# Two attentions of a language-model tower: where the softmax is divided, and how two value parts are added

## What is computed

```
first (8 heads of 16):   A = softmax(logits, axis=-1)
                         out = einsum("bhnm,bhmd->bhnd", A, V);  out @ Wo + bo
second (8 heads of 64):  s = einsum("qhd,khd->qhk", q / sqrt(64), k)
                         e = exp(s - max(s));  num = e @ v;  den = e.sum(-1)
                         (num / den) @ w_out + b_out
```

## Time and profile before

| | |
|---|---|
| Median of three runs | 1261.18 us |
| The profiled execution | 1261.07 us, its span 1258.9 us |
| TensorE matmul, weight load | 1057.9 us (84%), 810.6 us (64%) |
| VectorE | 1018.2 us (81%) |
| ScalarE | 694.7 us (55%) |
| GpSimd | 478.0 us (38%) |

### The profile page before, as it was taken

The page is one execution under the profiler, slowest core; times in us unless marked ns, Lnnn a source line. Parts: engine busy times, 40 slices in busy tenths (PEclk is TensorE's granted clock), DMA queues, the critical chain, the costliest instruction groups (busy, mean ns, idle before and its releaser), DMA issues.

```text
span 1258.9 us, 24020 instructions
## 1 busy us (share of the span) xinstructions
PE 1057.9 (84%) x7816; PEld 810.6 (64%) x7816; DVE 1018.2 (81%) x3131; ACT 694.7 (55%) x1481; POOL 478.0 (38%) x459
## 2 busy tenths in 40 slices
PE   5587787888869988988988886899898988989997
PEld 4455555565547877877887786465565655667665
DVE  5797887978899999999999982885875876844777
ACT  2686768878533443344434431784774865825333
POOL 6672552616505424244324422360551624600000
PEclk9699998989978999999999998999999999989999
DMA  3310000000000000000000002000000000000000
GB/s 109 113 51 1 1 0 0 0 0 1 1 1 2 2 2 1 2 2 2 2 2 2 1 3 116 1 2 1 0 0 0 0 0 1 1 1 1 1 9 24
DMA packets 6424, 14.36 MB, mean 11 GB/s; under 512 B 1855, under 2 KB 4482, under 8 KB 5762
## 3 DMA queue, kind: packets, MB, share of 16 engines
q1 hardware_dynamic: 5314, 11.16, 2.5%
q0 software_dynamic: 1024, 2.10, 0.7%
HBM read 12.20 MB, written 1.05 MB: 11 GB/s over the span
## 4 chain that ended last, share of the span: by engine, by line
PE 31%; issue 30%; DVE 28%; POOL 5%; ACT 4%; DVEq 1%; DMA 0%; POOLq 0%; SPq 0%; ACTq 0%
PE quad L1492 5%; PE bank L1487 4%; PE quad L1186 4%; DVE a_eT L750 4%; DVE w_v L1001 4%; DVE i L918 4%; PE quad L1198 3%; PE quad L1390 3%; PE bank L1401 2%; PE bank L1334 2%; DVE one_u L1007 2%; POOL a_en L380 2%; POOL wu L361 2%; DVE bi L939 1%; PE bank L1370 1%
## 5 line engine op out<-in xcount | busy, mean ns | idle before, releaser
L380 POOL TENSOR_TENSOR a_en<-a_e,a_rrec 128x512 f32<-128x512 f32 x256 | 265.2, 1040 | 324.6 <-DVE a_rrec L744 307.5
L464 ACT ACTIVATE a_e<-bank,a_negmax 128x512 f32<-128x512 f32 x256 | 176.1, 688 | 72.0 <-DVE a_negmax L737 62.0
L737 DVE TENSOR_REDUCE a_negmax<-bank 128x1 f32<-128x512 f32 x256 | 175.9, 690 | 40.8 <-PE bank L1427 25.2
L1186 PE MATMUL quad<-ident,a_en 128*128 128x128 f32 x1024 | 164.2, 284 | 47.9 <-DVE a_eT L750 40.9
L1186 PEld LDWEIGHTS quad<-ident,a_en 128*128 128x128 f32 x1024 | 111.3, 143 | 139.0 <-issue 121.5
L406 POOL TENSOR_TENSOR vals<-relu_in,g_sb 128x512 f32<-128x512 f32 x80 | 125.9, 1610 | 156.3 <-DVE one_u L1007 120.1
L750 DVE TENSOR_TENSOR a_eT<-quad,a_eT 128x512 fp32r<-128x512 f32 x256 | 172.4, 676 | 4.1 <-ACT a_eT L473 4.1
L1198 PE MATMUL quad<-a_eT,a_v 128*128 128x512 f32 x512 | 173.0, 428 | 1.7 <-DVE a_eT L750 1.7
L1370 PE MATMUL bank<-xnT,wd 128*128 128x128 f32 x1024 | 137.4, 291 | 34.3 <-ACT relu_in L569 34.0
L473 ACT CAST a_eT<-quad 128x512 fp32r<-128x512 f32 x256 | 147.8, 577 | 23.7 <-PE quad L1186 19.7
L1370 PEld LDWEIGHTS bank<-xnT,wd 128*128 128x128 f32 x1024 | 127.1, 201 | 42.7 <-ACT relu_in L569 42.4
(11 more groups left out here) (221 smaller groups left out, 1852.7 us busy)
## 6 DMA issues: line engine op xcount, KB each, us to landing
wd<-in_pk_down SPq DMA_DIRECT2D x1, 2048.0 KB, 8.0
wu<-in_pk_up SPq DMA_DIRECT2D x1, 2048.0 KB, 12.6
wu<-in_moe_w SPq DMA_DIRECT2D x2, 1024.0 KB
out<-h SPq DMA_DIRECT2D x4, 256.0 KB, 2.3
wd<-in_num_rows SPq DMA_DIRECT2D x1, 512.0 KB
q_st<-in_pk_wqT SPq DMA_DIRECT2D x1, 512.0 KB
q_st<-in_pk_keys SPq DMA_DIRECT2D x1, 512.0 KB
wd<-in_a_wk SPq DMA_DIRECT2D x1, 512.0 KB
```

Of the source, the lines that this page charges most:

```text
L380: nc.gpsimd.tensor_tensor(m.en[:, s % 3, :], m.e[:, s % 3, :], m.rrec[:, s % 4:s % 4 + 1].to_broadcast([P, S]), ALU.mult).then_inc(a.nr, 1)
L464: nc.scalar.activation(m.e[:, s % 3, :], bank[LOGITS[s % 3]][:, :], ACT.Exp, bias=m.negmax[:, s % 4:s % 4 + 1], accum_out=m.rowsum[:, s % ...
L737: V.tensor_reduce(m.negmax[:, s % 4:s % 4 + 1], bank[LOGITS[s % 3]][:, :], AX.X, ALU.max, negate=True).then_inc(a.mx, 1)
L1186: last = tp(bank[2 + s % 2][:, c * P:(c + 1) * P], m.en[:, s % 3, c * P:(c + 1) * P], ident[:])
```

## The change

In the first attention the exponentials are no longer divided. TensorE transposes `a_e` itself, so GpSimd's multiplication goes, and the inverse of each unit's sum too. The row sums of 16 units are kept side by side and inverted at once (twice a batch); GpSimd spreads the inverses over 32 columns per head (`spread_sums`), TensorE transposes them in four pieces (`transpose_sums`, bank 7 or 2), ScalarE copies them to SBUF (`copy_rT`), and VectorE multiplies them onto the output bank (`outT0`) in place of ScalarE's copy. A buffer `a_e` is now free when its transposition is done (`tr`).

In the second attention ScalarE copies the high and the low value part of a head apart, 64 partitions each, so that two heads lie in one tile of 128 rows; GpSimd adds the two parts (`add_parts`, four a batch), and `wo1` holds each row once: four products for each token block in place of eight.

```diff
@@ GpSimd
+            def spread_sums(b, g):
+                pool.wait_ge(a0.rc, 2 * b + g + 1)
...
+                nc.gpsimd.tensor_tensor(mB.rspread[:].rearrange("p j a n -> p a j n"), ...
+                                        ALU.mult).then_inc(r_spread, 1)
+            def add_parts(b, pair):
+                pool.wait_ge(a1.ots, b * H + 2 * pair + 2)
+                nc.gpsimd.tensor_tensor(oT1[:, pair, :], o_parts[:, pair % 2, 0, :], o_parts[:, pair % 2, 1, :],
+                                        ALU.add).then_inc(o_added, 1)
...
+            spread_sums(0, 0)
             with pool.Fori(0, B - 1) as b:
-                normalise(a0, b, lnB)
-            normalise(a0, B - 1)
+                rstd_step(lnB, b + 1, TPB)
+                spread_sums(b, 1)
+                spread_sums(b + 1, 0)
+            spread_sums(B - 1, 1)
             rstd_step(lnC, 0, TPB)
...
             normalise(a1, B - 1)
-            with pool.Fori(0, B) as b:
+            rstd_step(lnE, 0, TPB)
+            last_parts(B - 1)
+            for b in range(1, B):
                 rstd_step(lnE, b, TPB)
@@ ScalarE
                     if s >= 3:
-                        act.wait_ge(a.nr, b * UNITS + s - 2)
+                        act.wait_ge(a.tr if a is a0 else a.nr, b * UNITS + s - 2)
...
-                    nc.scalar.copy(a.oT[:, g, :], bank[4 + g % 2]).then_inc(a.ots, 1)
...
+                        rows = slice(g % 2 * DH1, (g % 2 + 1) * DH1)
+                        nc.scalar.copy(o_parts[rows, g // 2 % 2, 0, :], bank[4 + g % 2][0:DH1, :])
+                        nc.scalar.copy(o_parts[rows, g // 2 % 2, 1, :], bank[4 + g % 2][DH1:P, :]).then_inc(a.ots, 1)
...
+                    if a is a0 and s == HALF_UNITS + 5:
+                        copy_rT(b, 0)
@@ VectorE
+            def outT0(b, g):
+                dve.wait_ge(rT_sb, 2 * b + g + 1)
+                dve.wait_ge(a0.pv, b * UNITS + (g + 1) * HALF_UNITS)
+                V.tensor_tensor(oT0[:, g, :], bank[4 + g % 2], mB.rT[:], ALU.mult).then_inc(a0.ots, 1)
...
+                    if a is a0 and s in (HALF_UNITS + 1, UNITS + 1):
+                        invert_half(s // HALF_UNITS - 1)
+                    if a is a0 and s == HALF_UNITS + 9:
+                        outT0(b, 0)
@@ TensorE
-                    pe.wait_ge(a.nr, b * UNITS + s + 1)
+                    pe.wait_ge(a.ex if a is a0 else a.nr, b * UNITS + s + 1)
...
+                    if a is a0 and s == HALF_UNITS + 4:
+                        transpose_sums(b, 0)
+                    if a is a0 and s == UNITS + 4:
+                        pe.wait_ge(a.lo, b * UNITS + UNITS - 1)
+                        transpose_sums(b, 1)
...
-                    for g in range(a.groups):
+                    for g in range(a.groups if a is a0 else H // 2):
```

More of the change, by code:

```diff
@@ L453, in copy_xnT, with copy_rT @@
                                bank[7][:, 0:n]).then_inc(ln.sb, 1)
+            def copy_rT(b, g):
+                act.wait_ge(rT_ps, 2 * b + g + 1)
+                nc.scalar.copy(mB.rT[:], bank[R_BANK[g]][:, :]).then_inc(rT_sb, 1)
             def attention(a, b, next_ln=None, n=None, dst=None, tail=None, early_ln=None):
@@ L485, in attention @@
                     done = s - 8
-                    if done > 0 and done % (TPB * a.group) == 0:
+                    if a is not a0 and done > 0 and done % (TPB * a.group) == 0:
                         outT(done // (TPB * a.group) - 1)
+                    if a is a0 and s == HALF_UNITS + 5:
+                        copy_rT(b, 0)
                     if s == UNITS + 4 and next_ln is not None:
@@ L510, in heads0 @@
                 nc.scalar.activation(table_out[:, 0:1], ones[0:1, 0:1], ACT.Sqrt)
+                if before is not None:
+                    copy_rT(before, 1)
                 act.wait_ge(dev_rdy, b + 1)
@@ L755, in attention @@
                         rowmax(s)
-                    if 0 <= s - 1 < UNITS:
+                    if a is not a0 and 0 <= s - 1 < UNITS:
                         invert(s - 1)
+                    if a is a0 and s in (HALF_UNITS + 1, UNITS + 1):
+                        invert_half(s // HALF_UNITS - 1)
+                    if a is a0 and s == HALF_UNITS + 9:
+                        outT0(b, 0)
                     if drained is not None:
@@ L825, in heads0 @@
                 V.tensor_tensor(dev, q4, wide(0), ALU.subtract).then_inc(dev_rdy, 1)
+                if before is not None:
+                    outT0(before, 1)
                 dve.drain()
@@ L1174, in transpose_xn, with transpose_sums @@
                 last.then_inc(ln.ps, 1)
+            def transpose_sums(b, g):
+                pe.wait_ge(r_spread, 2 * b + g + 1)
+                for j in range(TPB):
+                    last = tp(bank[R_BANK[g]][:, j * P:(j + 1) * P], mB.rspread[:, j].rearrange("p a n -> p (a n)"), ident[:])
+                last.then_inc(rT_ps, 1)
             def attention(a, b, logits, next_ln=None, n=None, tail=None, early_ln=None, drained=None):
@@ L1293, in heads0 @@
                 pe.wait_ge(qkv_sb, b * TPB + TPB)
+                if before is not None:
+                    pe.wait_ge(rT_sb, 2 * before + 2)
                 for n in range(2 * H):
```

76 lines of the change are left out of this document (58 added, 18 removed).

## The result

The changed kernel took 1268.75 us (median of 7 runs) against 1260.43 for the kernel before in the same runs: ratio 1.0071, interval 1.0053 to 1.0089. Forecast were 1252 and "faster"; the time lies outside the range.

A forecast was written before the change was run, and what follows sets the result against it. It took as bounds a two-unit ring through VectorE's inverse in the first attention, not GpSimd's division, and TensorE in the second's projection. Terms -3.2 and -5.7 gave -8.9 on 1261.07, so 1252 us; range 1243 to 1262.

The forecast's parts named there:

- The copies of the second attention: Second attention's unit loop: ScalarE's second copy adds 0.35 a head in five heads a batch, +7.0 (4.2 to 11.8).
- The end of the last batch: Second attention's last projection: starts 1.7 later, so of the 4.0 saved only -1.0 is kept (-2.3 to +1).
- The queued power: Last batch, second attention: next layer norm's power, queued behind GpSimd's addition, puts the transposes between the quarters back.
- The projection between batches: Second attention's output projection: half the weight loads save 4.0 a batch, all on the path, -12.0 for three batches.
- hidden by the layer norm's statistics: Second attention, between batches: two more heads' second copies cost nothing there; the last costs 0.1 x 3 = +0.3.
- The first attention: All terms of the first attention together: -2.8 - 1.2 + 5.2 - 1.4 - 5.1 + 2.1 = -3.2.
- The second ring: First attention's unit loop: transposition, exponential three units on, high part, low part, transposition; 2.79 for two units, -2.8 in all.
- The idle time before the reduction into `k_aug`: First attention, batch to batch: VectorE's waits of 2.58 go as the output copy moves away; -5.1 net.
- the multiplication in the loop: First attention's loop: VectorE's output multiplication, 0.67, hardly hidden; part of the added work of 1.3 a batch, +5.2.
- C: Rival, second attention: each second copy costs its full 0.59 in all 32 heads; no change, 1264 us; chance 0.11.
- Rival B: First attention's unit loop: buffer returned by TensorE in order becomes the bound; 1.55 a unit, +16.8, 1269 us; chance 0.13.
- the second part's -5.7: All terms of the second attention together: -12.0 - 1.0 + 7.0 + 0.3 = -5.7.

The follow-up runs named there:

- e8: Second attention's change alone, with each head's two copies reading and writing the same 64 partitions; 1264.06 us, a single run.
- e9: e6 plus the second attention's change with one 128-partition copy a head, parts moved by DMA, e7's products and e10's order; 1245.36 us, ratio 0.9869.
- e7: Second attention's change alone, plus nine unread products keeping TensorE busy before the last projection; 1265.82 us, ratio 1.0058.
- e10: Second attention's change alone, with the next norm's power ahead of GpSimd's last addition instead of behind it; 1269.19 us, ratio 1.0059.
- e3: Changed kernel without the copy of the low value part, GpSimd adding the high part to itself (output lacks the low part); 1256.7 us, ratio 0.9949.
- e1: First attention's change alone, second attention as in the kernel before; 1260.94 us, ratio 0.9997.
- e5: e1 with the multiplication of the first half's output moved on VectorE from turn 25 to turn 33; 1255.93 us, ratio 0.9973.
- e6: e5 plus the product-key layer norm's power moved ahead of GpSimd's spreading of the last half's inverses; 1254.82 us, ratio 0.9964.

## Why the prediction was wrong

Its reading of what bounds the kernel held: GpSimd's division is not the bound, and its going earned nothing of itself. By its terms:

- **The copies of the second attention, +7.0 forecast, +11.4 measured.** This is the step that failed most by size inside the loop. It took 0.48 for the second copy, from two copies of 128 partitions, and 0.46 and 0.48 around it. The copies here change the first partition: the second starts 0.59 after the first, the exponential 0.61 after the second, and in odd heads the first copy 0.60 after the high part (0.47 in even heads). The copies of 64 rows beside the one that the text read (860.31) stood 0.60 apart. With the overlap kept (even heads of e8) the cost is 0.36 a head, where 0.35 was forecast. The upper bound of the text (11.8) did hold it.
- **The end of the last batch, -1.0 forecast, +4.1 measured.** "Of the 4.0 I keep -1.0" failed. The start is 2.9 later and not 1.7: TensorE's wait rose by 1.92, and the scaling beside GpSimd's addition costs 1.0 more (in e9, where the scaling is short, the start is 1.9 later). The larger omission was the granted clock behind a wait of 2.69: the blocks ran at the lower clock and none of the 4.0 was kept. e7 shows it: with the clock kept, the end is +0.5 and not +4.1. The queued power, which the text blamed, is not what cost the 4.0 (e10); with the clock kept it costs some 1.1 (e9's 6.87 against e7's 7.96).
- **The projection between batches, -12.0 forecast, -10.8 by its rows** (0.9 x 4 x 3): right. But the way from batch to batch kept only -6.6 of it, 1.4 less in each. Of this 1.0 is the scaling beside GpSimd's addition (2.08 instead of 1.12): the transposition behind it, and then the next queries, are 1.0 later (9.38 after the last exponential, 8.36 before). The text priced the additions at 0, by the divisions alone, though its own had a scaling lengthened by a GpSimd neighbour. The other 0.35 is a wait behind ScalarE's copies of the last heads, which I had "hidden by the layer norm's statistics"; with one copy (e3) that wait is gone. In e9 both are gone, and the way keeps all of the projection's 3.6.
- **The first attention, -3.2 forecast, 0 measured** (-2.6 to +1.8). The zero hides larger terms. In e1's trace against that of before, the units of the four batches take 7.8 more (187.3 against 179.4; forecast -0.2), the three ways to the next batch 8.4 less (85.2 against 93.6; forecast -5.1), and the end, from the last exponential to the first MAX8, 2.6 more (14.19 against 11.58; forecast +2.1). Units and ways are in part one: units 28 to 31 take 6.1 instead of 4.5 in the first three batches, and the way is counted from the last of them. The clock's falls differ between the two traces as well, so these are no exact prices. The second ring is there, with 2.85 for two units and not 2.79, so -2.8 became 0; two units in the timeline of the changed kernel:

```profile
150.39 0.42 PEld L1264 LDWEIGHTS quad<-ident,a_e 128*128 128x128 f32 x4 [0.57 <-issue]
...
151.15 0.69 ACT L506 ACTIVATE a_e<-bank,a_negmax 128x512 f32<-128x512 f32 x1 [0.23 <-PE quad L1264]
...
151.82 0.57 ACT L515 CAST a_eT<-quad 128x512 fp32r<-128x512 f32 x1
...
152.43 0.69 DVE L814 TENSOR_TENSOR a_eT<-quad,a_eT 128x512 fp32r<-128x512 f32 x1
```

Transposition to exponential 0.76, to the high part 0.67, to the low part 0.61, and 0.81 on to the next (low part 150.94, weights 151.75). I had 0.70 for the first. The idle time before the reduction into `k_aug` is gone, as forecast. The shorter times of e5 and e6 show that the 0.6 of the multiplication in the loop was rightly costed as uncovered.

The rivals: C, "each second copy costs its full 0.59", was the mechanism that came, in the five heads of the loop (11.4 for 20 heads, 0.57 each) and not in all eight, and it came with losses at the end and between the batches that no rival held. Rival B, the buffer returned by TensorE in order, holds in one place only, where a transposition stands behind a product that waits for the layer norm's copy, here in e1's timeline:

```profile
179.75 0.69 ACT L491 ACTIVATE a_e<-bank,a_negmax 128x512 f32<-128x512 f32 x1 [1.50 <-PE quad L1242]
```

The steady pace did not go to 1.55. The 0.73 for faster rested on the second part's -5.7, and there the bound for the end, +1, did not reach the +4.1 that came, since no bound had the lower clock or the longer scaling in it.

## What to carry to other kernels

A saving on an engine that waits anyway is only worth what its releaser leaves it: count first what the saving's own preparation (here two copies and an addition) puts on the engine that is nearly full, and what stands beside it on the other engines at that moment. Where work is made shorter behind a new wait of TensorE, price it at the lower clock as well. And an idea that loses may only have its helper on the wrong engine: with the parts moved by DMA, and with e6's first part (0.4% by itself) and e7's products, the same halved projection is faster than before by 1.3%.

## What the runs showed of the hardware

A ScalarE copy, or an exponential behind one, lay over the copy or cast of 512 columns before it by some 0.12 us only while the first partition stayed: 0.46 to 0.49 from start to start, against 0.59 to 0.62 where it changed from one half of the partitions to the other (e8, e3, the changed kernel and the query copies of before). The condition is read from the gaps of these kernels; why it holds, none of them shows. The Trainium skill ("ScalarE: Activation LUTs", "What ACT_TABLE_LOAD costs") gives an overlap of about 93 ns without this condition; the rows decide. VectorE's scaling of 4 x 128 x 128 floats took 1.12 us alone and 2.08 beside GpSimd's addition of 1.29, in each of the four batches. The DMAs of e9 that move 64 x 512 floats between partitions took 2.2 us from issue to landing (median); in the loop nobody waited for them, behind it only GpSimd did. A wait of TensorE of 2.0 to 2.2 in the first attention was followed by the lower clock in one trace of the changed kernel (granted 0.50 from 168.7 to 172.1 and from 339.4 to 342.8) and not in e1's; what decides there stays open.
